# Second layer of a two-layer block on one core: turning and low-rank projections of the next two batches moved beside the tail of the current two, expert rows gathered early

## The reference, cut to what matters

```python
# first layer, its end: two experts a token, rows of y picked by flat_idx
y_tok = y.reshape(E * B * cap, C)[flat_idx.reshape(-1)].reshape(B, T * K, C)
x = x + (y_tok * gates).reshape(B, T, K, C).sum(axis=2)      # "combine" in the kernel
# second layer, cond: low rank projections, weights differ by batch
w_down = down_project[None] * dg[:, None, :] + db[:, None, :]
w_up   = up_project[None] * ug[:, None, :] + ub[:, None, :]
h = x + relu(x @ w_down) @ w_up
# second layer, attention with random features (16 heads of 16, 64 features)
q, k = exp(feature(h @ Wq.T + bq)), exp(feature(h @ Wk.T + bk));  v = h @ Wv.T + bv
x = x + (q @ (k.T @ v)) / (q @ sum(k)) @ Wo.T + bo
# second layer, feed forward: a weight for each batch, then an int8 product by row scales
y = x @ weight[b] + bias[b];  s = max(abs(y)) / 127
x = x + (round(y / s) @ Wq8.T) * s * weight_scale + bias
```

## Time and profile before

| | |
|---|---|
| median of three runs | 2951.52 us |
| the profiled execution, its own time | 2960.49 us |
| span of the profile (first to last instruction) | 2958.6 us |
| mean granted TensorE clock | 0.808 |
| busy: TensorE, VectorE, ScalarE, GpSimd | 76%, 47%, 35%, 29% of the span |
| prologue of the second layer | 2336.8 to 2364.8 us of the span |
| bodies 1 to 4 | start at 2364.8, 2521.2, 2668.9 and 2822.5 us; the last instruction is at 2958.6 |

### The profile page before, as it was taken

One profiled execution on the slowest core, in us unless ns is written; L12 is line 12 of the kernel. 1 busy time (PEld: TensorE's weight loads), 2 busy tenths in 40 slices (PEclk: granted clock), 3 DMA queues, 4 the chain that ended last, 5 costly groups with the idle time before them and its releaser, 6 DMA issues. The chain is left out here.

```text
span 2958.6 us, 33480 instructions
## 1 busy us (share of the span) xinstructions
PE 2234.7 (76%) x11774; PEld 1408.6 (48%) x11774; DVE 1394.1 (47%) x3626; ACT 1026.0 (35%) x2535; POOL 858.4 (29%) x585
## 2 busy tenths in 40 slices
PE   6348887777778877777877778845999597878677
PEld 5224444444445444444544444524777454444444
DVE  2357566366465464565655643421111136363535
ACT  2015444343344343344334335411222142414242
POOL 0335253253252243334325421131000213232312
PEclk9578986787787678688588678766999789988889
DMA  6100100110020020020010010022222301010100
GB/s 219 38 16 1 53 29 1 55 41 1 32 64 1 15 74 8 15 74 8 15 60 22 15 50 22 15 64 93 97 96 96 96 16 46 28 45 28 43 31 15
DMA packets 62592, 128.54 MB, mean 43 GB/s; under 512 B 14564, under 2 KB 39258, under 8 KB 60130
## 3 DMA queue, kind: packets, MB, share of 16 engines
q1 hardware_dynamic: 46570, 76.19, 7.4%
q0 software_dynamic: 15872, 50.35, 5.6%
HBM read 97.04 MB, written 29.46 MB: 43 GB/s over the span
## 5 line engine op out<-in xcount | busy, mean ns | idle before, releaser
L1030 ACT ACTIVATE att_buf<-att_buf,nmin 128x384 f32<-128x384 f32 (+3 forms) x512 | 287.5, 562 | 720.6 <-DVE nmin L1345 714.5
L871 PE MATMUL bank<-kk,qT 32*128 32x512 f32 (+2 forms) x1024 | 348.4, 718 | 73.9 <-DVE nmin L1345 73.7
L703 POOL TENSOR_TENSOR big<-ex_at,kx 128x2048 f32<-128x2048 f32 x64 | 236.5, 3705 | 342.6 <-DVE xt_na L1139 268.8
L898 PE MATMUL bank<-ident,att_buf 128*128 128x128 f32 x1280 | 257.4, 340 | 47.2 <-ACT att_buf L1038 38.4
L1334 DVE TENSOR_TENSOR att_buf<-bank,wdiag 128x128 f32<-128x128 f32 x384 | 93.5, 284 | 330.1 <-PE bank L876 299.0
L912 PE MATMUL bank<-att_buf,vp 128*32 128x128 f32 x2560 | 234.7, 324 | 0.0
L649 POOL TENSOR_TENSOR big<-kx 128x1280 f32<-128x1280 f32 x64 | 162.6, 2567 | 244.2 <-ACT kx L970 237.9
L1038 ACT COPY att_buf<-bank 128x384 f32<-128x384 f32 (+3 forms) x512 | 208.8, 410 | 62.7 <-remote 36.9
L898 PEld LDWEIGHTS bank<-ident,att_buf 128*128 128x128 f32 x1280 | 186.6, 178 | 62.8 <-issue 36.1
L871 PEld LDWEIGHTS bank<-kk,qT 32*128 32x128 f32 x1024 | 116.0, 232 | 143.4 <-DVE nmin L1345 102.9
L912 PEld LDWEIGHTS bank<-att_buf,vp 128*32 128x32 f32 x2560 | 142.9, 127 | 64.7 <-issue 51.0
(11 more groups left out here) (342 smaller groups left out, 4005.8 us busy)
## 6 DMA issues: line engine op xcount, KB each, us to landing
ew<-in_eW SPq DMA_DIRECT2D x16, 1024.0 KB
buf_d<-zero SPq DMA_DIRECT2D x8, 640.0 KB, 7.9
er<-buf_d SPq DMA_DIRECT2D x8, 640.0 KB
y_d<-yy SPq DMA_DIRECT2D x8, 640.0 KB
xt_na<-in_xT SPq DMA_DIRECT2D x8, 512.0 KB, 3.5
nA<-in_xN SPq DMA_DIRECT2D x8, 512.0 KB, 4.3
x_d<-x SPq DMA_DIRECT2D x8, 512.0 KB, 3.4
kf<-x_d SPq DMA_DIRECT2D x8, 512.0 KB, 3.2
```

The source lines that it names most:

```text
L703: pool.tensor_tensor(pv[:, c * P:(c + 1) * P, :].rearrange("p (h d) o -> p o h d", d=DH), spread(ex[:, t, :, 8 * c:8 * c + 8], 3, DH), spr ...
L871: pe.matmul(bank[u % 2][:, 0:n], qT[r:r + 32, g, i * P:(i + 1) * P], kk[r:r + 32, g, T * i * P:T * i * P + n], start=True, stop=False)
L898: mm = pe.transpose(bank[3 + u % 2][:, j * P:(j + 1) * P], pr[:, u % NPR, j * P:(j + 1) * P], ident[:])
L1030: act.activation(pr[:, u % NPR, 0:n], pr[:, u % NPR, 0:n], ACT.Exp, scale=-1.0, bias=nmin[:, u % 4:u % 4 + 1], accum_out=rsum[:, i, h:h + ...
```

## The change

The head leaves the body. It becomes three functions that any block can place, with stages of their own (H_IN, H_DN, H_UP = ST_OT, ST_X3T, ST_Q), and that work in banks 0 and 1 of a lane only. The prologue runs them for the first two batches. A body with `more` runs them for the next two, behind the pieces of the two current lanes in the same stage. The tail's own transposes now use banks 2 and 3. `x2` and `yg` get memory of their own, `onT` and `x3T` replace the uses of `xT` and `hcT` in the tail. SP fetches the next gates, x and low-rank rows as soon as `xb` is made; row numbers are made at the start of ST_QK, the gathers are issued behind it, and the combine stands at the start of ST_V. The weights of the next head are made there too. The two loads of rows for the head move from the start of a body to that fetch.

```diff
+H_IN, H_DN, H_UP = ST_OT, ST_X3T, ST_Q
@@ buffers
-            v["yg"] = kff[:, 0:2 * T * D].rearrange("p (k t f) -> p k t f", k=2, f=D)
-            v["x2"] = tiled(kff[:, 2 * T * D:3 * T * D])
+            v["onT"] = v["qs"][:, 2:4, :]
+            v["x3T"] = v["kT"]
+            v["x2"] = v["x2"][:]
@@ in_stages
+            live = [p(n, lane_bufs[n], lambda name, n=n: s(f"{name}_{n}")) for p in programs for n in range(LANES)]
@@ new functions
+        def head_pe(pe, in_turn):
+            def lane(n, v, s):
+                bk = v["bank"]
+                yield H_IN
+                pe.wait_ge(s("x2_sum"), 2 * T)
+                if in_turn:
+                    pe.wait_ge(s("o_ok"), K2)
+                for m in range(K2):
+                    for t in range(T):
+                        mm = pe.transpose(bk[m][:, t * P:(t + 1) * P], v["x2"][:, t, m * P:(m + 1) * P], ident[:])
+                    mm.then_inc(s("xT_mm"), 1)
+                yield H_DN
+                pe.wait_ge(s("xT_ok"), 2)
+                pe.wait_ge(s("wud_ok"), 1)
+                for m in range(K2):
+                    mm = pe.matmul(bk[0][0:M, :], v["wdn"][:, m, :], v["xT"][:, m, :], start=(m == 0), stop=(m == K2 - 1))
+                mm.then_inc(s("dn_mm"), 1)
+                yield H_UP
+                pe.wait_ge(s("dn_ok"), 1)
+                for m in range(K2):
+                    pe.matmul(bk[m][:], v["wup"][:, m * P:(m + 1) * P], v["dT"][:], start=True, stop=True).then_inc(s("up_mm"), 1)
+            return lane
+        def head_act(act):
+            def lane(n, v, s):
+                bk = v["bank"]
+                yield H_IN
+                for m in range(K2):
+                    act.wait_ge(s("xT_mm"), m + 1)
+                    act.copy(v["xT"][:, m, :], bk[m][:]).then_inc(s("xT_ok"), 1)
+                yield H_DN
+                act.wait_ge(s("dn_mm"), 1)
+                act.activation(v["dT"][:], bk[0][0:M, :], ACT.Relu).then_inc(s("dn_ok"), 1)
+            return lane
+        def head_dve(dve):
+            def lane(n, v, s):
+                bk = v["bank"]
+                yield ST_V
+                dve.wait_ge(s("h_in"), 32)
...
+                dve.tensor_tensor(v["wup"][:], v["wup"][:], v["ugb"][:, 1, :], ALU.add).then_inc(s("wud_ok"), 1)
+                yield H_UP
+                for m in range(K2):
+                    dve.wait_ge(s("up_mm"), m + 1)
+                    dve.wait_ge(s("xT_ok"), 2)
+                    dve.tensor_tensor(v["hcT"][:, m, :], bk[m][:], v["xT"][:, m, :], ALU.add).then_inc(s("hc_ok"), 1)
+            return lane
@@ prologue: SP
                         fetch_rows(sp, lane_bufs[n], lane_sems[n], n)
+                        fetch_head(sp, lane_bufs[n], lane_sems[n], n)
@@ prologue: the head runs behind the combine on each engine
+                    in_stages(s, head_dve(dve))
+                    in_stages(s, head_pe(pe, False))
+                    in_stages(s, head_act(act))
@@ body: SP
-                                sp.wait_ge(s(f"kv_mm_{n}"), 1)
+                                sp.wait_ge(s(f"xb_ok_{n}"), 1)
                                 fetch_rows(sp, v, lambda name, n=n: s(f"{name}_{n}"), LANES * b2 + LANES + n)
+                                fetch_head(sp, v, lambda name, n=n: s(f"{name}_{n}"), LANES * b2 + LANES + n)
@@ body: GpSimd
-                            yield ST_UP
+                            yield ST_QK
                             pool.memset(v["kv"][:], 0.0).then_inc(s("kv0"), 1)
                             pool.memset(v["kd"][:], 0.0).then_inc(s("kv0"), 1)
                             pool.tensor_tensor(v["xb"][:], v["x2"], spread(row("bo"), 1, T), ALU.add).then_inc(s("xb_ok"), 1)
+                            yield ST_QK + 1
+                            if more:
+                                gather_rows(pool, v, s)
...
-                            yield ST_O
-                            if more:
-                                gather_rows(pool, v, s)
@@ body: TensorE, ScalarE, VectorE lose ST_IN, ST_DN and ST_UP; the end of each is
-                        in_stages(s, lane)
+                        in_stages(s, lane, *([head_pe(pe, True)] if more else []))
@@ body: VectorE
                             yield ST_QK
+                            if more:
+                                row_numbers(dve, v, s)
...
                             yield ST_V
+                            if more:
+                                combine(dve, v, s)
                             dve.wait_ge(s("v_mm"), 1)
...
                             yield ST_Y
-                            if more:
-                                combine(dve, v, s)
                             dve.wait_ge(s("yq_mm"), 1)
+                            dve.wait_ge(s("p_in"), 32)
```

More of the change, by code:

```diff
@@ L1577, in in_stages @@
                         due[n] = next(g, None)
[L1578 removed]
+            assert due == [None] * len(live)
         def fetch_rows(sp, v, s, b):
@@ L1616, in combine, with fetch_head @@
                                              ALU.mult, ALU.add).then_inc(s("x2_sum"), 1)
+        def fetch_head(sp, v, s, b):
+            for dst, src in ((v["dgb"][:].rearrange("p k h -> p (k h)"), spread(prow_d[b, PR["dg"][0]:PR["db"][1]], 0, P)),
+                             (v["ugb"][:].rearrange("p k h -> p (k h)"), spread(prow_d[b, PR["ug"][0]:PR["ub"][1]], 0, M))):
+                sp.dma_start(dst, src).then_inc(s("h_in"), 16)
+        def head_pe(pe, in_turn):
[20 more added lines that the diff above has]
+            return lane
@@ L1653, in _ @@
                         combine(dve, lane_bufs[n], lane_sems[n])
+                    in_stages(s, head_dve(dve))
+                @block.tensor
+                def _(pe):
+                    in_stages(s, head_pe(pe, False))
+                @block.scalar
+                def _(act):
+                    in_stages(s, head_act(act))
             s.clear()
@@ L1666, in _ @@
                             b = LANES * b2 + n
-                            for dst, src in ((v["dgb"][:].rearrange("p k h -> p (k h)"), spread(prow_d[b, PR["dg"][0]:PR["db"][1]], 0, P)),
-                                             (v["ugb"][:].rearrange("p k h -> p (k h)"), spread(prow_d[b, PR["ug"][0]:PR["ub"][1]], 0, M)),
-                                             (v["brow"][:], spread(prow_d[b, PR["bias"][0]:PR["bias"][1]], 0, P)),
+                            for dst, src in ((v["brow"][:], spread(prow_d[b, PR["bias"][0]:PR["bias"][1]], 0, P)),
                                              (v["wde"][:], wdec_d[b])):
@@ L1724, in tokens_major @@
                                 mm.then_inc(s(name), 1)
-                            yield ST_IN
-                            transposes(v["x2"], "xT_mm")
-                            yield ST_DN
-                            pe.wait_ge(s("xT_ok"), 2)
-                            pe.wait_ge(s("wud_ok"), 1)
-                            for m in range(K2):
-                                mm = pe.matmul(bk[2][0:M, :], v["wdn"][:, m, :], v["xT"][:, m, :], start=(m == 0), stop=(m == K2 - 1))
-                            mm.then_inc(s("dn_mm"), 1)
-                            yield ST_UP
-                            pe.wait_ge(s("dn_ok"), 1)
-                            for m in range(K2):
-                                pe.matmul(bk[m][:], v["wup"][:, m * P:(m + 1) * P], v["dT"][:], start=True, stop=True).then_inc(s("up_mm"), 1)
                             yield ST_QK
-                            pe.wait_ge(s("hc_ok"), 2)
                             for i in range(2 + 2 * K2):
@@ L1838, in lane @@
                             bk = v["bank"]
-                            yield ST_IN
-                            for m in range(K2):
-                                act.wait_ge(s("xT_mm"), m + 1)
-                                act.copy(v["xT"][:, m, :], bk[m][:]).then_inc(s("xT_ok"), 1)
-                            yield ST_DN
-                            act.wait_ge(s("dn_mm"), 1)
-                            act.activation(v["dT"][:], bk[2][0:M, :], ACT.Relu).then_inc(s("dn_ok"), 1)
                             yield ST_QK
@@ L1873, in lane @@
                                 act.wait_ge(s("qbT_mm"), m + 1)
-                                act.copy(v["qbT"][:, m, :], bk[m][:].bitcast(BF16)[:, 0:S]).then_inc(s("qbT_ok"), 1)
-                        in_stages(s, lane)
+                                act.copy(v["qbT"][:, m, :], bk[2 + m][:].bitcast(BF16)[:, 0:S]).then_inc(s("qbT_ok"), 1)
+                        in_stages(s, lane, *([head_act(act)] if more else []))
                     @block.vector
@@ L1985, in lane @@
                             dve.tensor_tensor(fo, fo, v["xb"][:], ALU.add).then_inc(s("fin"), 1)
-                        in_stages(s, lane)
+                        in_stages(s, lane, *([head_dve(dve)] if more else []))
                 s.clear()
```

38 lines of the change are left out of this document (14 added, 24 removed).

## The result

The changed kernel takes **2916.97 us** (median of 4 runs, 2908.64 to 2923.48), the kernel before 2955.72 (4 runs, 2951.47 to 2962.29): a ratio of 0.9865, 95% interval 0.9831 to 0.9900. The forecast was 2910, in a range of 2888 to 2938. The total was met within 7 us, but two errors of some 12 us lay in it with opposite signs.

The account below looks back on a forecast made before the run. Head and tail were taken as waiting chains, the tails lengthened by gathers that hold TensorE's handoffs. Prologue -2.8 and bodies -2.8, -8.3, -14.0, -13.2 sum to -41.1 us: 2910, range 2888 to 2938.

Parts of the forecast that it names:

- What bounds the kernel: Second layer: head and tail are waiting chains, TensorE bounds features, ScalarE ends ST_QK; gathers lengthen the tails.
- The hold: While GpSimd's gathers run, each handoff from TensorE costs about 2.7 us, one after the other.
- Gathers in ST_QK: Projections of bodies 1 to 3: seven handoffs held at 2.7 us delay ScalarE's restart; +3.4, then twice +4.4 us.
- sign of no hold: ScalarE's gap before lane 1's first q projection under 1.5 us would mean handoffs are not held in ST_QK.
- No hold in ST_QK: Rival, chance 0.16: ScalarE keeps its old start in the projections of bodies 1 to 3; 2893 us.
- ST_QK from a low clock: Projections start at 1.2 GHz after the pause: +2.5 us in bodies 2 to 4, nothing in body 1.
- ST_V: The v stage takes 15.5 us in bodies 1 to 3 and 13.9 in body 4, depending on TensorE's clock.
- Tail: Tails of bodies 1 to 3: 41.9 us without gathers and combine, plus 10.0 of head products, 51.9.
- heavier: Rival, chance 0.16: handoffs at 3.6 us, ST_V at 19.0, up product wholly at 1.2 GHz; 2938 us.
- Prologue: Ahead of body 1: the head's work partly beside the combine, so ST_QK starts earlier; -2.8 us.
- Combine and weights: In ST_V: they fall into VectorE's idle time or it catches up in features; nothing, otherwise 6 us a body.
- a sign of failure: Features stage growing past 38 us would mean VectorE or GpSimd did not catch up.

Follow-up runs that it names:

- experiment 8: Changed kernel with its 16 gathers a body issued at ST_O, not ST_QK + 1; they started in the k-v products (C): 3009.91 us.
- C: Chip (one set of runs) whose four traces all show "remote" waits; the kernel before took a median of 2953 us there.
- B: Chip (one set of runs) whose traces show no "remote" waits; the kernel before took a median of 2891 us there.
- A: Chip (one set of runs) whose traces show no "remote" waits; the kernel before took a median of 2890 us there.
- first comparison: The change against the kernel before, "remote" waits in both traces: 2916.97 us against 2955.72, ratio 0.9865.
- experiment 7: Norm products ahead of v's (C): on the kernel before 2938.53 us; on the best of experiment 6 2879.71; that plus 16 unused products a body 2887.89.
- experiment 4: The changed kernel, unchanged, against the kernel before on B: 2860.42 us, ratio 0.9892.
- experiment 6: Changed kernel, up product one stage earlier (A): 2861.85 us; down behind the batch's weight products, up right behind (B): 2824.09 us, ratio 0.9770.

## Why the forecast held, step by step

- **What bounds the kernel** was read rightly, with one omission. The hold was real in the two traces, and the gathers bring it on such a chip (experiment 8; on C tails with gathers in them take 54 to 55 us where B has 48.6, and tails without take 44.4 in both). It is more than a late count at each handoff: TensorE itself can be slow, at 2.7 instructions a microsecond in the k-v products of experiment 8. The slow starts do not explain the late counts, though: in body 1's projections TensorE ran without a gap until 2408.3, and ScalarE got the count at 2412.5. What links the two is open. The omission: how far a measured wait can belong to one chip. Nothing in one trace could tell.
- **Gathers in ST_QK**, the step that failed. I priced seven handoffs at 2.7 us each and so +3.4, and twice +4.4. ScalarE's restart before lane 1's first q projection, which it was to delay, came on time: the gap there is 1.33 us in all four bodies, under the 1.5 that the prediction had named as the sign of no hold. The hold struck later and once a body at most: a stall of 4.42 us in body 1, one of 2.91 in body 2 (felt only in v), none in body 3, 7.3 in sum where 12.2 were forecast. The projections are 48 instructions in 26 us, 1.9 a microsecond, less than the 2.7 that experiment 8 shows under gathers, so TensorE's starts are not slowed in them; the k-v products are 29. "No hold in ST_QK", held at 0.16, was nearer in bodies 2 and 3 (+1.7 and +2.3 measured, +2.5 by it, +6.9 by my case) and farther off in body 1 (+6.9 measured, 0 by it, +3.4 by my case).
- **The rule of the Trainium skill**, SBUF — State Buffer, "Who interferes with whom" (transfers never contend with a compute engine), gave that rival. On chips A and B the traces agree: 3.0 us of an ordinary wait for data. In the first comparison, with waits of up to 5.84 us, and on C, with 23 us in one stage, they don't. The measurement decides, and it decides by chip.
- **ST_QK from a low clock**: +2.5 forecast, 25.84 - 23.55 = 2.3 measured in body 4, and 2.0 to 2.7 in experiment 7 (22.7 to 23.4 against 20.7). Right. Body 1 should have paid nothing behind the prologue's products, but its first eight instructions took 6.20 us where eight at full clock take 3.60: 2.6 that were left out.
- **ST_V**: 15.5 forecast for three bodies; 14.75, 18.3 and 10.8 measured, and 10.8 for 13.9 in body 4. The mean was near, the price of each body not foreseeable from one trace: 10.8 to 20.5 us for the same instructions in the bodies of eleven traces.
- **Tail**: 51.9 forecast, 54.7 measured; transposes 1.91, down 3.65 as forecast. The mis-sized term is the up product: 7.2 us at 1.2 GHz throughout and 0.5 more for the int8 products (3.60, before 3.10), 7.7 and not 4.2. The whole tail is 2.8 us longer than forecast in each of three bodies, and I had named the full price as "heavier" only.
- **Prologue**: -2.8 forecast, -0.7 measured. The weights were waited for until 22.5 us after its start, before 18.4: 4.2 us more, where 2.0 were forecast. SP issued the last of the weights 3.0 us later than before (12.7 against 9.7 us after the start); the rest came in their landing.
- **Combine and weights** at nothing: right. VectorE is busy 3.25 us longer in ST_V, and the features stay at 36.5 us. Body 2's take 38.6, over the 38 that the prediction had named as a sign of failure, but not for VectorE: TensorE is busy for 38.2 of them, and the clock is 0.57 in their first 4.9 us.
- **Sum**: projections and v came out 12.3 us better than forecast, tails, prologue, pauses and features 11.6 us worse. Forecast -41.1, measured -41.8 in the profiles and 38.8 between the medians. The chance of 0.87 for "faster" rested on the heads, and these did go; that the total came within 7 us is luck, as the two errors cancel.
- **What the gain is made of.** This is worked out from the stages; neither half was run alone on a chip that holds. In the first comparison, moving the head gives -46.8 in front, +38.4 in the tails (3 x 12.8, from 54.7 - 41.9) and about +9 in the projections (9.1 on B, where nothing is held): nothing. Taking gathers and combine out of the tails gives -45.3 (171.0 less three times 41.9). On B the same sum gives the 19 us of experiment 4 nearly whole from the tails' 20 (three times 48.6 - 41.9); the rest of the 30 between the medians there is not assigned to either half, as v's clock differs from trace to trace. So the early fetch carries the change, and the head's move only becomes worth something when its products are put where TensorE waits: 31 us in experiment 6 by the tails (three times 10.3), 36 between the medians.

## What to carry to other kernels

Moving a chain off the front of a loop gained nothing here while it was put into another chain at its full length. Put into waits that the trace shows, its products gave two gains together: the filled wait and a higher clock (0.99, not 0.87). Where GpSimd issues gathers, put them under few long TensorE instructions (4.4, 2.9 and 0 us of stall here) rather than under many short ones (23 us a body), and look at the kernel on more than one chip before a wait is put down to the kernel. The same stage at 10.8 or 20.5 us is a reason to compare stage by stage, and not medians alone.

## What the runs showed of the hardware

- Chips differ in one thing and not in others: busy times agree within 1% (PE 2234.7 and 2214.2 us, ScalarE 1026.0 and 1023.3 for the kernel before), but under GpSimd's indirect transfers TensorE slows down in two of the four sets of runs and not in the others: on C to 56 instructions in 20.7 us, from 132 in 4.5.
- The clock fell from 2.4 to 1.2 GHz behind a wait of 2.7 us in some bodies and not in others of one execution, and in four bodies of experiment 7 without any wait, within or behind 32 back-to-back instructions of 8 columns. What decides between the two outcomes is left open here.
- Filling waits of 1.50 and 4.15 us in the tail was worth 10.3 us a body (54.7 to 44.4): TensorE's idle time there fell from 10.2 to 5.8 us, and its busy time from 44.4 to 38.6 at a clock of 0.99 and not 0.87.
